# A scatter-add into two tables in place of four, with four staging buffers kept

## What is computed

```python
h = relu(layernorm(x))
x = x + L0(h, src, dst, edge_attr)       # edge MLP, segment_sum over dst, node MLP
h = relu(layernorm(x))
x = x + L1(h)                            # hypergraph convolution over the same edges
# L1, in short (node_idx = src, he_idx = dst, 2,500 hyperedges):
he_feat = segment_sum(x_prime[node_idx], he_idx) * (hyperedge_weight / d_e)
out     = segment_sum(he_feat[he_idx], node_idx)      # the scatter of this case
out     = (out * d_v_inv_sqrt) @ W.T + b
```

## Time and profile before

| | us |
|---|---|
| median of three timed runs | 4982.13 |
| lowest, highest | 4980.34, 4989.26 |
| profiled execution: its span | 5038.3 |
| span less the median of the timed runs | 56.2 |
| share of the span: PE, DVE, POOL, ACT busy | 72%, 58%, 64%, 49% |

### The profile page before, as it was taken

One profiled execution on the slowest core, in us unless ns is written; L12 is line 12 of the kernel. 1 busy time (PEld: TensorE's weight loads), 2 busy tenths in 40 slices (PEclk: granted clock), 3 DMA queues, 4 the chain that ended last, 5 costly groups with the idle time before them and its releaser, 6 DMA issues. The chain is left out here.

```text
span 5038.3 us, 84982 instructions
## 1 busy us (share of the span) xinstructions
PE 3638.0 (72%) x16168; PEld 2611.6 (52%) x16168; DVE 2939.9 (58%) x8166; ACT 2492.2 (49%) x7380; POOL 3210.0 (64%) x2574
## 2 busy tenths in 40 slices
PE   3438999999999999999999997567633336666600
PEld 1216666666666666666666665565523324444300
DVE  6776776777777777767667775556811113323237
ACT  2437777777777777777777774462200001222200
POOL 2337777777777777777777774102366656888842
PEclk8665555555555555555555555555555555555555
DMA  6964444444444444444444442003311114555558
GB/s 249 343 242 113 117 117 112 115 114 114 117 112 116 113 116 115 114 114 115 111 112 113 116 113 61 12 15 95 101 49 47 44 38 80 75 74 78 74 124 222
DMA packets 726546, 557.03 MB, mean 111 GB/s; under 512 B 278174, under 2 KB 657170, under 8 KB 724594
## 3 DMA queue, kind: packets, MB, share of 16 engines
q0 software_dynamic: 135328, 250.63, 21.7%
q1 hardware_dynamic: 585138, 305.55, 21.4%
q10 hardware_dynamic: 6048, 0.52, 0.1%
HBM read 420.83 MB, written 135.45 MB: 110 GB/s over the span
## 5 line engine op out<-in xcount | busy, mean ns | idle before, releaser
L561 POOL DMA_INDIRECT stage<-p_tab,indices x1568 | 1761.6, 1123 | 660.3 <-issue 468.6
L674 ACT ACTIVATE table_weights_and_bias<-stage 128x256 bf16<-128x256 f32 x1568 | 632.4, 404 | 369.1 <-DVE stage L752 202.1
L768 DVE SCALAR_TENSOR_TENSOR stage<-stage,rstd,g 128x256 f32<-128x256 f32 x1568 | 653.9, 480 | 213.1 <-POOL rstd L567 213.1
L601 PE MATMUL ps_tiles<-edge_weights_a,edge_features_a 128*128 128x256 bf16 x1568 | 611.9, 390 | 201.1 <-DVE stage L752 156.4
L623 PE MATMUL ps_b<-window_mask,stage 128*128 128x32 f32 x3136 | 725.2, 402 | 2.9 <-ACT stage L680 2.9
L623 PEld LDWEIGHTS ps_b<-window_mask,stage 128*128 128x128 f32 x3136 | 698.3, 327 | 46.2 <-issue 43.3
L623 PE MATMUL ps_a<-window_mask,stage 128*128 128x32 f32 x3136 | 718.7, 400 | 1.9 <-ACT stage L680 1.7
L623 PEld LDWEIGHTS ps_a<-window_mask,stage 128*128 128x128 f32 x3136 | 706.8, 330 | 2.5 <-ACT stage L680 2.4
L602 PE MATMUL ps_tiles<-edge_weights_b,edge_features_b 64*128 64x256 bf16 x1568 | 614.4, 392 | 0.0
L752 DVE TENSOR_TENSOR stage<-ps_tiles,stage 128x512 f32<-128x512 f32 x784 | 538.1, 687 | 104.6 <-issue 101.2
L680 ACT ACTIVATE stage<-stage 128x1024 f32<-128x1024 f32 x392 | 414.2, 1057 | 366.8 <-DVE stage L774 332.5
(11 more groups left out here) (258 smaller groups left out, 5413.2 us busy)
## 6 DMA issues: line engine op xcount, KB each, us to landing
edge_features_a<-ea_part SPq DMA_DIRECT2D x784, 64.0 KB
ea_part<-sums SPq DMA_DIRECT2D x42, 896.0 KB, 5.5
sums<-ea_d SPq DMA_DIRECT2D x14, 1792.0 KB, 9.2
stage<-p_tab,indices POOLq DMA_INDIRECT x1568
edge_features_b<-ea_part SPq DMA_DIRECT2D x392, 64.0 KB
acc<-zeros_bf SPq DMA_DIRECT2D x392, 64.0 KB
sums<-acc SPq DMA_DIRECT2D x56, 448.0 KB
sums<-src_d SPq DMA_DIRECT2D x46, 512.0 KB
```

Source lines behind the costliest of these rows:

```text
L561: gp.indirect_dma_start(out=rows[:, j, :], out_offset=None, in_=k.p_tab[:, :], in_offset=bass.IndirectOffsetOnAxis(ap=k.meta[h][:, j:j + 1 ...
L601: nc.tensor.matmul(psH[q][:, t, :], k.eaA[h][:, e:e + P], k.wA[:, :], start=True, stop=False)
L674: nc.scalar.activation(k.scratch[:, j % GROUP, :], z[h][:, j, :], ACT.Square, scale=HID ** -0.5, accum_out=k.ssq[i][:, at:at + 1]).then_in ...
L768: o(v.scalar_tensor_tensor(z[h][:, j, :], z[h][:, j, :], root, k.g1[:, :], ALU.mult, ALU.mult))
```

## The change

`SCATTER_TABLES` goes from 4 to 2; a new constant `STAGED = 4` keeps four staging buffers. A scatter of tile n goes into table n % 2 and waits for scatter n - 2. A buffer is given back by a new semaphore `s_back`, which POOL raises after that wait and ahead of the scatter; since the wait says that scatter n - 2 has landed, copy n of ACT waits for a count of n + 1 (two are given at the start), that is, for POOL to have passed the wait of scatter n - 2, behind which scatter n - 4 has landed.

```diff
-SCATTER_TABLES = 4
+SCATTER_TABLES = 2
+STAGED = 4
...
 # scatter_rows, POOL
-            for r in range(R):
-                gp.dma_start(k.acc[r][NP:NP + P, :], summed[:, r, :]).then_inc(s_sc[r], 16)
+            for t in range(T):
+                gp.dma_start(k.acc[t][NP:NP + P, :], summed[:, R - T + t, :]).then_inc(s_sc[t], 16)
+            gp.sem_inc(s_back, STAGED - T)
...
-                    wait_apart(k, gp, s_sc[r], 16 * (BODY // R * b + n // R) + 16)
-                    gp.indirect_dma_start(out=k.acc[r], out_offset=bass.IndirectOffsetOnAxis(
+                    wait_apart(k, gp, s_sc[n % T], 16 * (BODY // T * b + n // T) + 16)
+                    gp.sem_inc(s_back, 1)
+                    gp.indirect_dma_start(out=k.acc[n % T], out_offset=bass.IndirectOffsetOnAxis(
                         ap=k.target[h][:, j:j + 1], axis=0), in_=summed[:, r, :], in_offset=None,
-                        compute_op=ALU.add).then_inc(s_sc[r], 16)
+                        compute_op=ALU.add).then_inc(s_sc[n % T], 16)
...
 # scatter_rows, ACT
             def take_rows(b, n):
                 r = n % R
                 a.wait_ge(s_ps, BODY * b + n + 5)
-                a.wait_ge(s_sc[r], 16 * (BODY // R * b + n // R) + 16)
+                a.wait_ge(s_back, BODY * b + n + 1)
                 a.copy(summed[:, r, :], ps[n % 2][:, 0:D]).then_inc(s_c, 1)
```

More of the change, by code:

```diff
@@ L1639, in scatter_rows @@
     s_sz = k.sem("sc_zeros")
+    s_back = k.sem("sc_rows_given_back")
     s_free = k.sem("sc_targets_used")
-    R = SCATTER_TABLES
+    R, T = STAGED, SCATTER_TABLES
     PB, PH = BODY // 2, HALF // 2
@@ L1710, in _ @@
                     wait_apart(k, gp, s_c, BODY * b + n + 3)
-                    wait_apart(k, gp, s_sc[r], 16 * (BODY // R * b + n // R) + 16)
-                    gp.indirect_dma_start(out=k.acc[r], out_offset=bass.IndirectOffsetOnAxis(
+                    wait_apart(k, gp, s_sc[n % T], 16 * (BODY // T * b + n // T) + 16)
+                    gp.sem_inc(s_back, 1)
+                    gp.indirect_dma_start(out=k.acc[n % T], out_offset=bass.IndirectOffsetOnAxis(
                         ap=k.target[h][:, j:j + 1], axis=0), in_=summed[:, r, :], in_offset=None,
-                        compute_op=ALU.add).then_inc(s_sc[r], 16)
+                        compute_op=ALU.add).then_inc(s_sc[n % T], 16)
                     if j == R - 1:
                         gp.sem_inc(s_free, 1)
-            for r in range(R):
-                wait_apart(k, gp, s_sc[r], 16 * (BODY // R) * n_bodies + 16)
+            for t in range(T):
+                wait_apart(k, gp, s_sc[t], 16 * (BODY // T) * n_bodies + 16)
         @block.tensor
@@ L1826, in far_scatter @@
     s_sz = k.sem("far_zeros")
+    s_back = k.sem("far_rows_given_back")
     rows = k.stage[:, 0:HALF * D].rearrange("p (j d) -> p j d", d=D)
     at = HALF * D
-    summed = k.stage[:, at:at + SCATTER_TABLES * D].rearrange("p (j d) -> p j d", d=D)
+    summed = k.stage[:, at:at + STAGED * D].rearrange("p (j d) -> p j d", d=D)
     src_row = [k.U[:, i * HALF * P:(i + 1) * HALF * P].bitcast(I32).rearrange("p (j e) -> p j e", e=P)
```

## The result

The changed kernel takes **5038.92 us** (median of 4 runs, 5036.75 to 5041.31) against 4981.24 for the kernel before beside it (4 runs, 4979.17 to 4989.26): ratio 1.0112 over all runs (1.0116 by the medians), 95% interval 1.0097 to 1.0127. It is slower by 57.7 us. The direction and the range of the prediction held; its +118 us is a little over twice what came. The profiled span went from 5038.3 to 5035.0 us, so the two profiled executions show no loss at all, and their stages are to be compared one by one.

A forecast was written before the change was run, and what follows sets the result against it. Stages run one after another; POOL paces the scatter stage, DMA loads, DVE and stores the output loop, PE the edge stage. 156 (scatter waits) + 4 - 42 = +118 on 4982 gave 5100 us, range 5010 to 5155.

The forecast's parts named there:

- The regular steps: Scatter stage: each scatter waits for scatter n - 2, landing 3.39 plus release 0.91 gives 4.30 us a step: +88 us.
- The price of an increment: Scatter stage: one semaphore increment between release and scatter was taken to cost 0.10 us.
- release free: Rival, scatter stage: release costs only 0.30, regular steps lose nothing, slow landings still cost: +30 us, 5012; chance 10%.
- landing shorter: Rival, scatter stage: with fewer transfers in flight the landing shortens and never binds: -42 us, 4940; chance 5%.
- The slow landings: Scatter stage: about 40 landings delayed by SP's 512 KB load, no longer hidden, cost 1.7 us each: +68 us.
- the rival in which a load hits two scatters of a half: Scatter stage: release costs 1.12 and the load delays two scatters per half: +151 to +219 us; chance 12%.
- Far scatter: Far scatter: two groups of 8 scatters, three extra pair steps of about 0.6 us each: +4 us.
- output stage: Output stage: two of five loads go and adds fall from three to one, 17.1 for 22.8 us: -42 us.
- The zero rows: Edge stage: 196 zeroing DMAs of 64 KB less, costed at nothing as hidden behind PE.
- The -20 kept for the range: Edge stage: allowance of -20 us if SP were late for something, up to 2.4 us a body.
- The sum's own execution: Whole kernel: terms were summed against a profiled execution of 5038.3 us, 1.1% longer than the timed median.

The follow-up runs named there:

- f3: Changed kernel with one increment less between the wait for the table and the scatter: 5012.62 us, ratio 1.0019 to the kernel before.
- e0: The kernel before, unchanged, run once more for its profile on another chip: 4787.88 us.
- e1: Changed kernel with four tables zeroed in the edge stage as before, on a chip without pauses: 4885.08 us, ratio 1.0204 to the kernel before.
- e3: Changed kernel with a second 512 KB load in every half of the scatter stage: 4895.87 us, ratio 1.0222 to the kernel before.
- e2: Kernel before with only tables 0 and 1 zeroed in the edge stage, 2 and 3 later from ACT's queue: 4788.71 us, ratio 1.0001.
- g1: Kernel before with two zero rows in the edge stage, the others issued by ACT in the hyperedge stage: 4788.25 us, ratio 1.0000.
- h1: Kernel before with only tables 0 and 1 zeroed in the edge stage, run again: ratio within 0.9998 to 1.0003.
- i1: Kernel before with only tables 0 and 1 zeroed in the edge stage, another repeat: ratio within 0.9998 to 1.0003.
- i2: Kernel before with only tables 0 and 1 zeroed in the edge stage, one more repeat: ratio within 0.9998 to 1.0003.
- i3: Kernel before with no zero row in the edge stage, all issued by ACT in the hyperedge stage: ratio within 0.9998 to 1.0003.
- f2: Changed kernel with four tables zeroed in the edge stage, on a chip with pauses: 5100.98 us, ratio 1.0186 to the kernel before.
- f1: The changed kernel as it is, run again on a chip with pauses: 5025.29 us, ratio 1.0046 to the kernel before.
- g4: Changed kernel with no zero row in the edge stage, all issued by ACT in the hyperedge stage: 4881.41 us, ratio 1.0193 to the kernel before.

## Why the prediction was right or wrong

*The regular steps (+88): right, a little large.* The step from n - 2 to n is 4.22 us in the median of regular places, not 4.30: 159.5 x 4.22 = 673.1, less 598.3, is +74.8. (One of the bounds was worked out wrong: 0.81 for the release gives 159.5 x 4.20 = 669.9, +72 and not +69.) The price of an increment was about right (0.10 taken, 0.07 to 0.09 by f3). The landing stayed where it was: the copies no longer show it, but the view of the scatter's line gives its median as 3.4 us with four tables (e0) and 3.3 with two (e1). With 3.39 the start after a release was 4.22 - 3.39 = 0.83, the increment included, and not 0.81 + 0.10. By the Trainium skill ("DMA: Bandwidth & Descriptors", Anatomy of one DMA) the estimated landing of 2.15 us would have left the step at 3.72; the measured 4.22 disagrees. So the rivals "release free" (3.72) and "landing shorter" fell as well.

*The slow landings (+68): right in size.* 738.1 - 673.1 = 65.0, and not the 136 of the rival in which a load hits two scatters of a half. They come at the scatter two later and its neighbour, once in a half. e3 shows that a second load right behind the first adds 11 us and not 65, so counting them by halves was the right unit for this kernel.

*Far scatter (+4) and output stage (-42): right*, at +4.4 and -44.0, the latter by its three parts.

*The zero rows (0): this step failed.* It read: "I cost this at nothing, hidden behind PE". PE busy 0.93 of the stage was taken for PE being the bound; but 0.93 of 2740 leaves 197 us of idle PE, and I asked neither where they came from nor what the 377 us of DVE without a releaser were. Both views were there. The argument that no engine waits for SP's loads was true (but for 6 us of PE, once) and did not bear on it: what the zero rows cost is the wait of DVE for a signal of PE that comes 2 to 4 us late, later beside four issues than beside two. The term is 0 on the chips without pauses (e2, g1, h1, i1 and i2 on four of them; on the fifth i3, which has no zero row in the edge stage at all), -75.7 timed by f2 and f1, and about -42 in the first series (57.7 less the 99.9 of the other stages). The -20 kept for the range named the right place, but for SP being late and not for DVE, and doesn't follow from the "up to 2.4 us a body" beside it, which is 235 us over 98 bodies; 75.7 us are 0.8 a body.

*The sum's own execution.* The profiled executions of the first series put this term at -108, since the one of the kernel before ran 57 us over its timed median and the one of the changed kernel 4 us under. That the 56 us stood beside the median in the table was noted in the prediction and not used: with an execution that far off, some stage of it must be longer than in the timed runs, and it was likely this one, as far as the other stages tell (for one and the same kernel they agree within 10 us over all batches, but for the hyperedge gathers, 466 us here against 405 on chips without pauses).

Without the zero rows the change measures +97.2 (e1), +100.1 (f2) and +92.9 (g4), each against the kernel before on its own chip; the forecast for that was +118. The changed kernel itself was not run on a chip without pauses; e1 and g4 stand in for it there.

## What to carry to other kernels

An engine that is busy 93% of a stage bounds it only if its idle 7% cannot be bought back: divide the stage by its number of bodies and name what fills each body, above all idle time of another engine for which the profile names no releaser; the code says what it waits for, and the timeline whether that was done in time. Taking half of the tables away trades a landing hidden four scatters deep for one on the path: landing plus release (3.39 + 0.83) against two issues (3.72) decides it, before any slow landing is counted. And measure a change of issues on more than one chip, since here the two kernels differ by 0.5% in one series, by 1.1% in another and, with e1 and g4 in the changed kernel's place, by 2%.

## What was not expected of the hardware

The kernel before, at the same clock, takes some 4788 us on five chips and 5001 on one. For one kernel (e1 and f2) the edge stage is 2554 against 2714 us and the hyperedge stage 405 against 468. In f2's edge stage DVE starts its mask 3.16 us (median) after the matmul that it waits for, in e1's always 0.04. It is alike in the hyperedge stage: DVE's add of the sums (L1585) starts up to 8.7 us after its matmul in f2, at most 0.23 in e1. How many zero rows SP issues changes the length of DVE's wait (4.54 against 2.84 us in one body, 349.8 against 270.8 over the stage). The trace doesn't say what holds the signal up, and no run settled it.
